# Local attention and a mixture of experts: the scores as split passes, with VectorE making the low parts

## The chip, the cores and the metric

One Trainium2 chip, one of its cores. The metric is the device time of the kernel in microseconds (us), the median of several runs.

## What is computed

x is 4 x 1024 tokens of width 512 in float32. A block of local attention with 8 heads of 128 and windows of 128 tokens is added to x and normalised; then 2 of 8 experts and a shared one are applied and normalised. Cut to the part that the change touches:

```python
q = _l2norm(q) * q_scale
k = _l2norm(k) * k_scale
kw, vw = (look_around(kb), look_around(vb))        # the window before, and this one
sim = jnp.einsum('bhnid,bhnjd->bhnij', qb * SCALE, kw)
sim = jnp.where(mask, sim, jnp.finfo(sim.dtype).min)
attn = jax.nn.softmax(sim, axis=-1)
o = jnp.einsum('bhnij,bhnjd->bhnid', attn, vw).reshape(b, H, n, DH)
```

## The kernel before

The 4096 tokens are 32 tiles of 128 tokens, each one window of the attention. Phase A (`in_steps`) runs 35 steps. In step s tile s is projected (`project`: q0, k0, q1, k1, v0, v1, each 4 heads wide, and the gates z), tile u = s-1 goes through the attention in two groups g of 4 heads, tile w = s-2 is projected out and normalised, and tile s-3 is routed. Steps 4 to 31 are a hardware loop of two steps a turn; 31 steps (1 to 31) both project and attend. Phase B then runs the experts over tiles of gathered tokens (`tile_steps`), with 64 indirect scatters of routing records on GpSimd (`scatter_records`) and 72 gathers and 72 scatters of rows.

Each engine has its own list of instructions in program order and waits on semaphores; no scheduler reorders them. The order inside a step is written out by hand in each engine's `step` function.

The projections are split: an operand a is ah + al, both in the type fp32r, and a product is three matmuls (ah,wh), (ah,wl), (al,wh) that add up in one bank (L980, and L1071 for the output). The scores (L1035) are one matmul of plain float32 a head instead, the transposed q standing (128x128) and the k of two windows moving (256 columns); the trace shows each as two records.

The path of a group of scores: VectorE scales q and k by their norms into `qkn` (`scale`, L1209), TensorE transposes 4 heads of q into bank psT[0] and 4 of k into psT[1] (`turn_qk`, L1021), ScalarE copies them into SBUF with the q scale (`heads_T`, L750 and L755), each copy raising `trev`, and TensorE's `scores` waits for

```python
                pe.wait_ge(trev, 4 * u + 2 * g + 2)
```

VectorE then adds the mask and takes the maximum (`mask_max`, L1222). The norms of the new tile run beside it on the same engines: ScalarE squares a projected bank (`squares`, L743), VectorE sums and clamps it (`sums`, L1197 and L1202), GpSimd raises it to -1/2 (`power`, L600), VectorE scales (`scale`).

TensorE's list in a full step is: project q0, turn_qk of group 0, gates (L992, 8 matmuls of 16 columns), router (L1005, 8 of the same), scores of group 0, project_out, turn_qk of group 1, project k0, scores of group 1, project q1 and k1, turn_p, project v0, values, turn_p, project v1, values, turn_x2. VectorE's is: sums and scale of q0, the router's logits, the gate sums (`add_gate`, L1255 and L1257), mask_max and gate_scale of group 0, the residual and its normalisation, sums of k0, mask_max of group 1, scale of k0, then q1 and k1, and the low parts of the output.

Of the kernel before, what the change touches and what calls it, by code (L numbers as in the profile page):

```python
# [50 lines left out]
def block_kernel(nc, x, xT, wqkvT, woT, wgT, bg, qs, ks, gateT, w13T, w2T, out):  # L51
# [7 lines left out]
    with ExitStack() as ctx:  # L59
# [3 lines left out]
        def sbuf(stack, name, shape, dt=F32):  # L63
# [47 lines left out]
        qT = sbuf(sa, "qT", [P, H, P])  # L111
        kT = sbuf(sa, "kT", [P, 2, H, P])
# [18 lines left out]
                 kT[:, :, :, :].rearrange("p s h d -> p (s h d)").rearrange("p (c n) -> p c n", n=GRP)]  # L131
# [78 lines left out]
        tr_s = sem("tr_s")  # L210
        trev = sem("trev")
# [495 lines left out]
        def _(act):  # L707
# [37 lines left out]
            def heads_T(u, g, par, middle):  # L745

                act.wait_ge(tr_s, 4 * u + 2 * g + 1)
                if middle or u >= 1:
                    act.wait_ge(sim_s, 4 * (u - 1) + 2 * g + 2)
                act.activation(qT[:, g * HPG:(g + 1) * HPG, :], psT[0][:, :], ACT.Copy, scale=qks[:, 0:1])\  # L750
                   .then_inc(trev, 1)
                act.wait_ge(tr_s, 4 * u + 2 * g + 2)
                if not middle and u == 0 and g == 0:
                    act.wait_ge(w_lo, NW)
                act.activation(kT[:, par, g * HPG:(g + 1) * HPG, :], psT[1][:, :], ACT.Copy).then_inc(trev, 1)  # L755
# [129 lines left out]
        def _(pe):  # L885
# [139 lines left out]
            def scores(u, g, first):  # L1025
                pe.wait_ge(trev, 4 * u + 2 * g + 2)
                if first and g == 0:
                    pe.wait_ge(kv_clear, 2)
                for b in range(2):
                    if not (first and g == 0):  # L1030

                        pe.wait_ge(masked, 8 * u + 4 * (g - 1) + 2 * b + 2)
                    for hh in range(2):
                        h = g * HPG + 2 * b + hh
                        mm = pe.matmul(psS[b][:, hh * 2 * P:(hh + 1) * 2 * P], qT[:, h, :], kT[:, :, h, :],  # L1035
                                       start=True, stop=True)
                    mm.then_inc(sim_s, 1)
# [121 lines left out]
        def _(dve):  # L1159
# [52 lines left out]

            def mask_max(u, g, upar, first):
# [45 lines left out]
            def first_tile():  # L1259
# [12 lines left out]
                dve.memset(kT[:, 1, :, :], 0.0).then_inc(kv_clear, 1)  # L1272
# [12 lines left out]
            def step(s, par, middle=False):  # L1285
# [18 lines left out]
                if attn_on:  # L1304
                    mask_max(u, 0, 1 - par, u_first)
                    gate_scale(u, 0, u_first)
# [11 lines left out]
                if attn_on:  # L1318
                    mask_max(u, 1, 1 - par, u_first)
# [262 lines left out]
```

## Time and profile before

| what | value |
|---|---|
| median of 3 runs | 1885.11 us (1884.11 to 1886.3) |
| span of the profiled execution | 1878.1 us |
| median less that span | 7.0 us |
| mean granted TensorE clock | 0.958 of full |
| phase A, full steps | about 60 to 1140 us of the span, 35.1 us a step |
| phase B | from about 1180 us to the end |
| score groups | 64, of 4 heads each |

The profiled execution has no time of its own beside its span; 7.0 us lie between the span and the median. A start in a timeline is in us from the start of the span, and the next figure is the duration of the row. Matmuls are pipelined and their ends are modelled, so the distance between two starts says more of a matmul's cost than its duration. What follows "<-" in brackets is what ended the idle time before a row. PE is TensorE, DVE is VectorE, ACT is ScalarE, POOL is GpSimd, SP is SyncE.

### The profile page before, as it was taken

Reading aid. Unit: us, or ns where it says so; the run is one execution under the profiler, and the core shown is the slowest. Engines: PE = TensorE matmul, PEld = TensorE weight load, DVE = VectorE, ACT = ScalarE, POOL = GpSimd, SP = SyncE. Lnnn points to the kernel's source line nnn. Section 1 sums busy time; section 2 is a strip of 40 time slices with the busy share of each in tenths; the row PEclk is TensorE's granted clock in tenths of the full one; section 3 lists DMA queues with packets and bytes.
Section 4 is the critical chain, followed back from the end, with each engine's and each line's share of the span. In section 5 each row is a group of like instructions: output and inputs, shape, how many; then the busy total and the mean of one; then the engine's idle time right before and its main releaser. Section 6 shows DMA issues by size and latency. Waiting matters only on the chain.

```text
span 1878.1 us, 28855 instructions
## 1 busy us (share of the span) xinstructions
PE 1696.8 (90%) x8566; PEld 1362.8 (73%) x8567; DVE 769.8 (41%) x1893; ACT 660.2 (35%) x1525; POOL 600.2 (32%) x689
## 2 busy tenths in 40 slices
PE   6999999999999999999999997652899999999960
PEld 4888888888888888888888886431567777777640
DVE  5444444444444444444444443621422222222386
ACT  4334334334333333333333332211323333333332
POOL 3332232232232232232232231275024444444111
PEclk8999999999999999999999998886999999999995
DMA  6000000000000000000000002452743333333697
GB/s 215 7 18 29 23 17 28 22 17 28 22 17 28 22 17 28 22 17 28 22 17 28 22 17 74 140 96 55 239 145 101 103 104 101 101 102 105 227 334 245
DMA packets 81976, 139.92 MB, mean 75 GB/s; under 512 B 10428, under 2 KB 27396, under 8 KB 81940
## 3 DMA queue, kind: packets, MB, share of 16 engines
q1 hardware_dynamic: 66852, 101.54, 16.9%
q0 software_dynamic: 13600, 37.90, 6.3%
q8 instruction: 18, 0.29, 0.1%
q10 hardware_dynamic: 1488, 0.04, 0.0%
q14 instruction: 18, 0.15, 0.0%
HBM read 97.89 MB, written 41.56 MB: 74 GB/s over the span
## 4 chain that ended last, share of the span: by engine, by line
PE 82%; issue 9%; DMA 3%; DVE 3%; ACT 1%; POOL 1%; another core or an unknown queue 0%; SPq 0%; POOLq 0%; ACTq 0%; DVEq 0%
PE bank L980 29%; PE bank L919 12%; PE bank L1071 9%; PE bank L948 7%; PE bank L1059 6%; PE bank L1035 6%; PE bank L1048 3%; PE bank L1021 3%; PE bank L894 2%; PE bank L1005 2%; PE bank L992 1%; PE bank L929 1%; DMA fs<-in_w13T 1%; DMA bx<-x_d 1%; PE bank L1078 1%
## 5 line engine op out<-in xcount | busy, mean ns | idle before, releaser
L980 PE MATMUL bank<-wh,xh 128*128 128x512 f32 x768 | 324.6, 423 | 17.7 <-DVE wl L1169 11.6
L980 PE MATMUL bank<-wl,xh 128*128 128x512 f32 x768 | 306.8, 399 | 0.0
L980 PE MATMUL bank<-wh,xl 128*128 128x512 f32 x768 | 305.1, 397 | 0.0
L600 POOL TENSOR_TENSOR rnorm<-ssmax,nhalf 128x4 f32<-128x4 f32 x128 | 131.2, 1025 | 519.9 <-DVE ssmax L1202 516.7
L606 POOL TENSOR_TENSOR pp<-pp,gs 128x1024 f32<-128x1024 f32 x64 | 121.3, 1895 | 225.9 <-DVE gs L1241 225.9
L980 PEld LDWEIGHTS bank<-wh,xh 128*128 128x128 f32 x768 | 145.9, 190 | 52.2 <-issue 11.3
L760 ACT ACTIVATE pp<-pp,nmx 128x256 f32<-128x256 f32 x256 | 127.3, 500 | 128.3 <-DVE nmx L1227 128.3
L980 PEld LDWEIGHTS bank<-wh,xl 128*128 128x128 f32 x768 | 145.8, 190 | 35.9
L743 ACT ACTIVATE sq<-bank 128x512 f32<-128x512 f32 x128 | 76.7, 599 | 257.1 <-PE bank L980 257.1
L980 PEld LDWEIGHTS bank<-wl,xh 128*128 128x128 f32 x768 | 146.4, 191 | 28.2
L1197 DVE TENSOR_REDUCE ssum<-sq 128x4 f32<-128x512 f32 x128 | 87.8, 686 | 135.6 <-ACT sq L743 132.8
L1188 DVE TENSOR_TENSOR bl<-bank,bh 128x512 fp32r<-128x512 f32 x104 | 71.8, 691 | 174.0 <-ACT bh L737 165.1
L948 PE MATMUL bank<-w2e,gT 128*128 x288 | 135.2, 592 | 0.0
L1059 PEld LDWEIGHTS bank<-pT,vv 128*128 128x128 f32 x1024 | 125.5, 194 | 9.9 <-ACT pT L769 4.7
L1209 DVE TENSOR_TENSOR qkn<-bank,rnorm 128x512 f32<-128x512 f32 x128 | 88.5, 692 | 106.7 <-POOL rnorm L600 106.7
L1059 PE MATMUL bank<-pT,vv 128*128 128x128 f32 x1024 | 126.4, 277 | 4.2 <-ACT pT L769 4.2
L1488 DVE TENSOR_TENSOR gg<-bank,gg 128x256 f32<-128x256 f32 x104 | 44.1, 424 | 205.9 <-ACT gg L867 166.1
L1246 DVE TENSOR_TENSOR ol<-bank,oh 128x512 fp32r<-128x512 f32 x64 | 44.3, 692 | 201.3 <-ACT oh L775 201.3
L1035 PE MATMUL bank<-kT,qT 128*128 128x256 f32 x512 | 123.9, 385 | 2.2 <-ACT kT L755 2.0
L894 PEld LDWEIGHTS bank<-ident,bx 128*128 128x128 f32 x416 | 52.4, 145 | 96.0 <-DMA bx<-x_d 48.6
L670 POOL DMA_INDIRECT eo_d<-eo,dstc x72 | 72.2, 1003 | 148.8 <-ACT eo L872 138.4
L775 ACT ACTIVATE oh<-bank 128x512 fp32r<-128x512 f32 x64 | 38.3, 599 | 230.6 <-PE bank L1059 230.6
(181 smaller groups left out, 3355.5 us busy)
## 6 DMA issues: line engine op xcount, KB each, us to landing
fs<-in_w13T SPq DMA_DIRECT2D x18, 512.0 KB
xt<-in_xT SPq DMA_DIRECT2D x33, 256.0 KB, 3.1
xr<-in_x SPq DMA_DIRECT2D x32, 256.0 KB, 2.7
x_d<-xr SPq DMA_DIRECT2D x32, 256.0 KB, 2.0
bx<-x_d SPq DMA_DIRECT2D x32, 256.0 KB
ga<-eo_d SPq DMA_DIRECT2D x16, 512.0 KB, 5.4
gb<-eo_d SPq DMA_DIRECT2D x16, 512.0 KB, 6.2
out<-oo SPq DMA_DIRECT2D x32, 256.0 KB, 2.7
```

Source lines behind the costliest of these rows:

```text
L600: pool.tensor_tensor(rnorm[:, :], ssmax[:, :], nhalf[:, :], ALU.pow).then_inc(rn_s, 1)
L606: pool.tensor_tensor(pp[:, g * HPG:(g + 1) * HPG, :], pp[:, g * HPG:(g + 1) * HPG, :], gs[:, g * HPG:(g + 1) * HPG].unsqueeze(2).to_broadc ...
L760: ins = act.activation(pp[:, h, :], pp[:, h, :], ACT.Exp, bias=nmx[:, h:h + 1], accum_out=esum[:, h:h + 1])
L894: mm = pe.transpose(bank[par][:, c * P:(c + 1) * P], bx[:, par, c * P:(c + 1) * P], ident[:, :])
L919: mm = pe.matmul(bank[2 + par][:, :], a[:, par, c, :], b[:, c, :], start=(c == 0 and k == 0), stop=(c == DC - 1 and k == 2))
L948: mm = pe.matmul(bank[6 + par][:, :], gT[:, par, m, :], w2[:, m, :], start=(m == 0), stop=(m == IC - 1))
L980: mm = pe.matmul(b[:, :], a[:, par, c, :], wt[:, c, cols], start=(c == 0 and k == 0), stop=(c == DC - 1 and k == 2))
L1035: mm = pe.matmul(psS[b][:, hh * 2 * P:(hh + 1) * 2 * P], qT[:, h, :], kT[:, :, h, :], start=True, stop=True)
L1059: mm = pe.matmul(psO[:, hh * P:(hh + 1) * P], vv[:, k, g * HPG + hh, :], pT[:, hh, k * P:(k + 1) * P], start=(k == 0), stop=(k == 1))
L1071: mm = pe.matmul(psY[:, :], a[:, h, :], b[:, h, :], start=(h == 0 and k == 0), stop=(h == H - 1 and k == 2))
L1197: dve.tensor_reduce(ssum[:, :], sq[:, :].rearrange("p (h d) -> p h d", d=P), AX_X, ALU.add)\
L1209: dve.tensor_tensor(qkn[:, j, :].rearrange("p (h d) -> p h d", d=P), psA[j % 2][:, :].rearrange("p (h d) -> p h d", d=P), rnorm[:, :].unsq ...
```

## The change

q and k are kept as a high and a low part of type fp32r. ScalarE's two copies now write the high parts (`qTh`, `kTh`) and raise `qk_hi`; a new function of VectorE, `heads_low`, computes the low parts from the same banks and the high parts, and raises `trev`, on which TensorE waits as before. A head's scores are three matmuls in one bank. `heads_low` stands ahead of `mask_max` in both groups. For room, the scratch for the descriptors of GpSimd's DMAs (`dynamic_dma_scratch_size`) is set to 4096 bytes, and a staging buffer that lay over kT now lies over kTh.

```diff
--- before.py
+++ after.py
@@ -108,8 +108,13 @@
         ssmax = sbuf(sa, "ssmax", [P, HPG])
         rnorm = sbuf(sa, "rnorm", [P, HPG])
         qkn = sbuf(sa, "qkn", [P, 4, GRP])
-        qT = sbuf(sa, "qT", [P, H, P])
-        kT = sbuf(sa, "kT", [P, 2, H, P])
+        qTh = sbuf(sa, "qTh", [P, H, P], F32R)
+        qTl = sbuf(sa, "qTl", [P, H, P], F32R)
+        sk = ExitStack()
+        passing_k = sbuf(sk, "passing_k", [P, DC, GRP])
+        sk.close()
+        kTh = sbuf(sa, "kTh", [P, 2, H, P], F32R)
+        kTl = sbuf(sa, "kTl", [P, 2, H, P], F32R)
         vv = sbuf(sa, "vv", [P, 2, H, P])
         pp = sbuf(sa, "pp", [P, H, 2 * P])
         mx = sbuf(sa, "mx", [P, H])
@@ -128,7 +133,7 @@
 
 
         stage = [pp[:, :, :].rearrange("p h (a c) -> p (h a c)", c=GRP // 2).rearrange("p (c n) -> p c n", n=GRP),
-                 kT[:, :, :, :].rearrange("p s h d -> p (s h d)").rearrange("p (c n) -> p c n", n=GRP)]
+                 passing_k[:, :, :]]
         stage += [passing[:, i, :, :] for i in range(4)]
         sa.close()
 
@@ -208,6 +213,7 @@
         ez_s = sem("ez_s")
         v_s = sem("v_s")
         tr_s = sem("tr_s")
+        qk_hi = sem("qk_hi")
         trev = sem("trev")
         sim_s = sem("sim_s")
         mask_s = sem("mask_s")
@@ -747,12 +753,12 @@
                 act.wait_ge(tr_s, 4 * u + 2 * g + 1)
                 if middle or u >= 1:
                     act.wait_ge(sim_s, 4 * (u - 1) + 2 * g + 2)
-                act.activation(qT[:, g * HPG:(g + 1) * HPG, :], psT[0][:, :], ACT.Copy, scale=qks[:, 0:1])\
-                   .then_inc(trev, 1)
+                act.activation(qTh[:, g * HPG:(g + 1) * HPG, :], psT[0][:, :], ACT.Copy, scale=qks[:, 0:1])\
+                   .then_inc(qk_hi, 1)
                 act.wait_ge(tr_s, 4 * u + 2 * g + 2)
                 if not middle and u == 0 and g == 0:
                     act.wait_ge(w_lo, NW)
-                act.activation(kT[:, par, g * HPG:(g + 1) * HPG, :], psT[1][:, :], ACT.Copy).then_inc(trev, 1)
+                act.activation(kTh[:, par, g * HPG:(g + 1) * HPG, :], psT[1][:, :], ACT.Copy).then_inc(qk_hi, 1)
 
             def exps(u, g):
                 act.wait_ge(nmx_s, 2 * u + g + 1)
@@ -1032,8 +1038,9 @@
                         pe.wait_ge(masked, 8 * u + 4 * (g - 1) + 2 * b + 2)
                     for hh in range(2):
                         h = g * HPG + 2 * b + hh
-                        mm = pe.matmul(psS[b][:, hh * 2 * P:(hh + 1) * 2 * P], qT[:, h, :], kT[:, :, h, :],
-                                       start=True, stop=True)
+                        for k, (a, w) in enumerate(((qTh, kTh), (qTh, kTl), (qTl, kTh))):
+                            mm = pe.matmul(psS[b][:, hh * 2 * P:(hh + 1) * 2 * P], a[:, h, :], w[:, :, h, :],
+                                           start=(k == 0), stop=(k == 2))
                     mm.then_inc(sim_s, 1)
 
             def turn_p(u, g):
@@ -1209,6 +1216,22 @@
                 dve.tensor_tensor(qkn[:, j, :].rearrange("p (h d) -> p h d", d=P),
                                   psA[j % 2][:, :].rearrange("p (h d) -> p h d", d=P),
                                   rnorm[:, :].unsqueeze(2).to_broadcast([P, HPG, P]), ALU.mult).then_inc(scaled, 1)
+
+            def heads_low(u, g, upar, first):
+
+                heads = slice(g * HPG, (g + 1) * HPG)
+                dve.wait_ge(qk_hi, 4 * u + 2 * g + 1)
+                if not first:
+                    dve.wait_ge(sim_s, 4 * (u - 1) + 2 * g + 2)
+                if first and g == 0:
+                    dve.wait_ge(qks_s, 1)
+                dve.scalar_tensor_tensor(out=qTl[:, heads, :].rearrange("p h d -> p (h d)"), in0=psT[0][:, :],
+                                         scalar=qks[:, 0:1], in1=qTh[:, heads, :].rearrange("p h d -> p (h d)").bitcast(F32),
+                                         op0=ALU.mult, op1=ALU.subtract).then_inc(trev, 1)
+                dve.wait_ge(qk_hi, 4 * u + 2 * g + 2)
+                dve.tensor_tensor(kTl[:, upar, heads, :].rearrange("p h d -> p (h d)"), psT[1][:, :],
+                                  kTh[:, upar, heads, :].rearrange("p h d -> p (h d)").bitcast(F32), ALU.subtract)\
+                   .then_inc(trev, 1)
 
             def mask_max(u, g, upar, first):
                 for b in range(2):
@@ -1269,7 +1292,8 @@
                 weight_low(7)
 
                 dve.wait_ge(w_lo, NW)
-                dve.memset(kT[:, 1, :, :], 0.0).then_inc(kv_clear, 1)
+                dve.memset(kTh[:, 1, :, :].bitcast(F32), 0.0)
+                dve.memset(kTl[:, 1, :, :].bitcast(F32), 0.0).then_inc(kv_clear, 1)
                 dve.wait_ge(consts, 11)
 
             def layernorm_stats(src, n, bn, m, v, prev):
@@ -1302,6 +1326,7 @@
                 if proj_on:
                     add_gate(s)
                 if attn_on:
+                    heads_low(u, 0, 1 - par, u_first)
                     mask_max(u, 0, 1 - par, u_first)
                     gate_scale(u, 0, u_first)
                 if out_on:
@@ -1316,6 +1341,7 @@
                 if proj_on:
                     sums(s, 1)
                 if attn_on:
+                    heads_low(u, 1, 1 - par, u_first)
                     mask_max(u, 1, 1 - par, u_first)
                 if proj_on:
                     scale(s, 1, attn_on)
@@ -1569,7 +1595,7 @@
         "w13T": w13.transpose(0, 2, 1),
         "w2T": w2.transpose(0, 2, 1),
     }
-    nc = _bacc.Bacc("TRN2", target_bir_lowering=False, num_devices=1)
+    nc = _bacc.Bacc("TRN2", target_bir_lowering=False, num_devices=1, dynamic_dma_scratch_size=4096)
     arrays, args = {}, []
     for name in _INS:
         arr = _np.ascontiguousarray(laid[name])
```

VectorE's list at group 0 of a middle step, before (`logits`, `zt` and `zb` are the router's copy and the gate sums, `pp` the masked scores):

```order
L1209 TENSOR_TENSOR qkn<-bank,rnorm 128x512
L1299 REGISTER_ALU
L1300 ISA
L1300 COPY logits<-bank 128x16
L1252 ISA
L1255 TENSOR_TENSOR zt<-bank,bgb 128x8
L1256 REGISTER_ALU
L1257 TENSOR_TENSOR zb<-bank,zt 128x8
L1217 ISA
L1218 ISA
L1222 ISA pp,mx<-bank,mask 128x256
```

and of the change:

```order
L1216 TENSOR_TENSOR qkn<-bank,rnorm 128x512
L1323 REGISTER_ALU
L1324 ISA
L1324 COPY logits<-bank 128x16
L1275 ISA
L1278 TENSOR_TENSOR zt<-bank,bgb 128x8
L1279 REGISTER_ALU
L1280 TENSOR_TENSOR zb<-bank,zt 128x8
L1225 ISA
L1228 SCALAR_TENSOR_TENSOR qTl<-bank,qks,qTh 128x512
L1231 REGISTER_ALU
L1232 TENSOR_TENSOR kTl<-bank,kTh 128x512
```

The two low parts stand behind the scaling of the new tile's q0 and behind the gate sums.

VectorE's list at group 1 of the same step, before (`xr` is the normalised residual, `ssum` and `ssmax` the sum and clamp of k0's squares):

```order
L1314 TENSOR_SCALAR xr<-xr,mv,rstd 128x512
L1194 REGISTER_ALU
L1197 TENSOR_REDUCE ssum<-sq 128x4
L1202 TENSOR_SCALAR ssmax<-ssum 128x4
L1215 REGISTER_ALU
L1217 REGISTER_ALU
L1218 REGISTER_ALU
L1222 ISA pp,mx<-bank,mask 128x256
```

and of the change:

```order
L1339 TENSOR_SCALAR xr<-xr,mv,rstd 128x512
L1201 REGISTER_ALU
L1204 TENSOR_REDUCE ssum<-sq 128x4
L1209 TENSOR_SCALAR ssmax<-ssum 128x4
L1223 REGISTER_ALU
L1225 REGISTER_ALU
L1228 SCALAR_TENSOR_TENSOR qTl<-bank,qks,qTh 128x512
L1231 REGISTER_ALU
L1232 TENSOR_TENSOR kTl<-bank,kTh 128x512
L1241 REGISTER_ALU
```

Here they stand behind the sum and the clamp of k0's squares.

## Rows read from the trace of the kernel before

**Rows 1.** The profile's page: the span, and busy time of each engine
```profile
span 1878.1 us, 28855 instructions
...
PE 1696.8 (90%) x8566; PEld 1362.8 (73%) x8567; DVE 769.8 (41%) x1893; ACT 660.2 (35%) x1525; POOL 600.2 (32%) x689
```

**Rows 2.** The page's chain that ended last, by engine
```profile
PE 82%; issue 9%; DMA 3%; DVE 3%; ACT 1%; POOL 1%; another core or an unknown queue 0%; SPq 0%; POOLq 0%; ACTq 0%; DVEq 0%
```

**Rows 3.** One step: us, busy of PE, PEld, DVE, ACT, POOL, clock, DMA share, GB/s
```profile
636.54:671.65 35.11, 35.11 (x197) 30.18 (x196) 15.85 (x46) 13.43 (x34) 10.22 (x9) 1.00 0.07 23
```

**Rows 4.** Timeline of TensorE in that step (start, duration of the row, instructions)
```profile
636.54 1.04 PE L1021 MATMUL bank<-ident,qkn 128*128 128x128 f32 x8
637.33 0.26 PE L992 MATMUL bank<-wgp,xh 128*128 128x16 f32 x1
637.44 0.26 PE L992 MATMUL bank<-wgp,xl 128*128 128x16 f32 x1
...
639.12 1.97 PE L1035 MATMUL bank<-kT,qT 128*128 128x256 f32 x8
...
650.08 1.89 PE L1035 MATMUL bank<-kT,qT 128*128 128x256 f32 x8
...
652.04 0.41 PE L980 MATMUL bank<-wl,xh 128*128 128x512 f32 x1
652.28 0.39 PE L980 MATMUL bank<-wh,xl 128*128 128x512 f32 x1
...
661.18 1.95 PE L1059 MATMUL bank<-pT,vv 128*128 128x128 f32 x16
662.97 1.04 PE L1048 MATMUL bank<-ident,pp 128*128 128x128 f32 x8
```

**Rows 5.** Timeline of VectorE, the same step
```profile
637.45 0.69 DVE L1197 TENSOR_REDUCE ssum<-sq 128x4 f32<-128x512 f32 x1 [2.02 <-ACT sq L743]
...
639.58 0.69 DVE L1209 TENSOR_TENSOR qkn<-bank,rnorm 128x512 f32<-128x512 f32 x1 [1.24 <-POOL rnorm L600]
640.19 0.16 DVE L1300 COPY logits<-bank 128x16 f32 x1
...
640.46 0.17 DVE L1257 TENSOR_TENSOR zb<-bank,zt 128x8 f32<-128x8 f32 x1
...
651.80 0.17 DVE L1202 TENSOR_SCALAR ssmax<-ssum 128x4 f32<-128x4 f32 x1
```

**Rows 6.** Timeline of ScalarE, the same step
```profile
636.82 0.60 ACT L743 ACTIVATE sq<-bank 128x512 f32<-128x512 f32 x1 [1.64 <-PE bank L980]
...
637.89 0.60 ACT L755 ACTIVATE kT<-bank 128x512 f32<-128x512 f32 x1
...
650.44 0.60 ACT L743 ACTIVATE sq<-bank 128x512 f32<-128x512 f32 x1 [2.16 <-PE bank L980]
```

**Rows 7.** Timeline of TensorE around holes; in brackets the idle before a row
```profile
18.07 0.56 PE L980 MATMUL bank<-wh,xh 128*128 128x512 f32 x1 [1.09 <-DVE zb L1257]
...
22.05 0.40 PE L980 MATMUL bank<-wl,xh 128*128 128x512 f32 x1
...
28.10 0.50 PE L980 MATMUL bank<-wh,xh 128*128 128x512 f32 x1 [2.61 <-DVE qkn L1209]
...
32.32 0.40 PE L980 MATMUL bank<-wh,xl 128*128 128x512 f32 x1
...
1144.58 3.64 PE L1059 MATMUL bank<-pT,vv 128*128 128x128 f32 x16 [3.44 <-ACT pT L769]
...
1221.05 0.66 PE L894 MATMUL bank<-ident,bx 128*128 128x128 f32 x4 [2.87 <-DMA bx<-x_d]
...
1304.30 0.69 PE L929 MATMUL bank<-ident,gg 128*128 128x128 f32 x2 [28.85 <-issue]
```

**Rows 8.** Timeline of GpSimd and of SyncE, last scatter and the read behind
```profile
1300.13 0.96 POOL L644 DMA_INDIRECT slot_d<-rec,slot_u  x1 [0.30 <-issue]
...
1361.33 0.44 SPq L527 DMA_DIRECT2D slot_t<-slot_d  x1
```

## The prediction

> **What bounds the kernel now.** I read the page's first lines first: the span is 1878.1 us and TensorE is busy for 90% of it [rows 1]. The chain that ended last is TensorE for 82% [rows 2]. An average hides which stage is full, so I cut out one step of phase A, from the transposes of one step (636.54) to those of the next (671.65). In these 35.11 us TensorE is busy for 35.11 us at the full granted clock, while VectorE has work for 15.85 us, ScalarE for 13.43 and GpSimd for 10.22 [rows 3]. So phase A is bounded by TensorE alone, with no hole in it: what is taken from TensorE shortens the kernel one for one, and every wait put on it lengthens it one for one. VectorE at 45% seems to have room. Room on average is not enough; what counts is when VectorE gets to the new work, so the last view is the step in order of time on TensorE, VectorE and ScalarE [rows 4 to 6].
>
> **Part 1: the scores on TensorE.** A group of 4 heads is now eight records of plain float32. From 650.08 to the second matmul behind it, 652.04, are 1.96 us; less the 0.24 between that one and its neighbour [rows 4], a group costs about 1.72 us. The change makes it 12 matmuls of 256 columns, each with its own load of the stationary side. No row shows this shape. From below: 16 weight-loaded float32 passes of 128x128 take 1.79 us (661.18 to 662.97), 0.112 each, and matmuls of only 16 columns still come 0.11 apart (637.33, 637.44) [rows 4], so a loaded matmul isn't faster than 0.11. From above: split matmuls of 512 columns come 0.24 apart; half their columns less is 0.107 less at 2.4 GHz, which gives 0.13. (The crude upper end, that 256 columns cost the same 0.24 as 512, would be 2.9 us a group.) I take 0.12: 1.44 us a group, a gain of 0.28, over 64 groups 18 us; with the ends 0.11 and 0.13, 26 and 10 us.
>
> The Trainium skill (TensorE: Matmul & The Clock Gate, Back-to-back issue gap) gives N/2.4 + 2.5 ns between warm matmuls, 109 ns for 256 columns. By it a group would take 1.31 us and the gain would be 26 us, 8 us more than I take; the rows show 0.24 where this rule gives 0.216 for 512 columns, so I stay with the rows.
>
> **Part 2: VectorE's two low parts, on the path.** Here lies the price. Before, the matmuls of scores waited for ScalarE's two copies only. The k copy of group 0 ended at 638.49 [rows 6], 0.63 us ahead of the scores at 639.12 [rows 4]. Now they wait for VectorE as well, and VectorE is in order: the two new instructions stand behind everything that its list has before them.
>
> Group 0: ahead of them stand the sum and the scaling of the new tile's q0 and the two gate sums. q0's squares start at 636.82 on ScalarE [rows 6], the sum at 637.45, GpSimd's power lies between, the scaling starts at 639.58, the last gate sum at 640.46 [rows 5]. So the low part of q starts at about 640.6. Its duration isn't in the trace for this operation; the nearest row is the subtraction or product over a bank of 512 columns (the scaling, 0.69 us, and the instruction behind it starts 0.61 after it, at 640.19) [rows 5]. The k part then ends at 640.6 + 0.61 + 0.69 = 641.9, and the scores start at 641.95 in place of 639.12: TensorE stands for 2.83 us.
>
> Group 1: ahead stand the sum and the clamp of k0's squares. TensorE ends k0 just as it wants the scores (650.08); the squares start at 650.44 [rows 6], the clamp at 651.80 [rows 5]. The low parts take from 651.95 to 653.22, the scores start at 653.27: 3.19 us.
>
> Both waits hang on a projection that TensorE ended just before, so they don't shrink as the step grows: the chain starts when TensorE ends q0 or k0. Nor do they hide behind other TensorE work, as it takes its list in order. What is queued behind the new VectorE instructions: the masks wait for the scores anyhow; the scaling of k0 comes later, but the third projection (q1, 2.8 us) lies between the scores and k1, which needs it. The two extra clears at the first tile cover themselves: VectorE idled before the next sum. The copies and the added DVE time (4 x 0.65 us a step) load nobody else. Low parts from above: if the product-and-subtract costs twice the subtraction, 0.7 more a group, 43 us; from below, no less than the 0.69 of a bank read of any kind, so 0.
>
> **Part 3: the clock.** TensorE's holes were none; now there are two a step. What a hole does is read from elsewhere in the trace. After 2.61 us of standing (28.10) eleven intervals take until 32.32, 4.22 us, where at the upper level they would take 11 x 0.24 = 2.64: the clock fell to 1.2 GHz and cost about 1.55. Behind the small gate matmuls and a hole of only 1.09 us (18.07) ten intervals last until 22.05: 3.98 for 2.40, again 1.55. After 3.44 us the sixteen records of 1144.58 take 3.64, where the same sixteen at 661.18 take 1.95. But after 2.87 us (1221.05) the four transposes behind it take 0.66, full speed [rows 4, 7]. Group 0's hole follows upon 1.8 us of those same small matmuls, so I count 1.55 for each; group 1's follows dense work, where the rows go both ways, more often down: 1.1.
>
> **Part 4: the smaller DMA scratch.** It holds GpSimd's descriptors. The last of the 64 record scatters starts at 1300.13, and what they wrote is read at 1361.33 [rows 8]: should they wait for the smaller scratch, there are 60 us of cover. Yet while they ran TensorE stood for 28.85 us until 1304.30, put down to "issue" [rows 7]. I can't say what of it hangs on the scratch: 0 taken, with a bound of 29 us either way.
>
> **Sum.** A step of the 31 that both project and attend: 2.83 + 3.19 of waits, 1.55 + 1.1 of clock, 2 x 0.28 gained: +8.1 us, 251 us in all. The last attention step has no projections: its two groups wait one more VectorE instruction each, 2 x 0.7, less 0.56: +1. Span 1878.1 + 252 = 2130. The median of the runs, 1885.11, is 7.0 above the profiled span, which I take as what lies around it; the forecast is **2137 us**, about 13% slower.
>
> **The rivals.**
> (a) The waits come, the clock holds, as behind the hole of 1221.05: 31 x 2.65 = 82 us less, 2055. For it: that row, and that dense work stands on both sides. Against: three of the four holes under 4 us [rows 7]. Chance 0.15.
> (b) The other side: VectorE reaches the low parts in time, and the gain of part 1 is all there is. Point of decision: both must be done by 639.1 and 650.1, so started by 637.8 and 648.8. Then 1885 - 18 = 1867. Against: the scaling alone starts at 639.58, and the order of VectorE's list puts it first. It needs a reordering that the built program doesn't have. Chance 0.03.
> (c) Each of the 12 loads lies bare: 0.107 of columns plus the 0.11 of a load is 0.22 a matmul, 2.6 us a group, 0.9 more than now; against my sum 64 x 1.17 = 75 us more, 2212. Against: in the 512-column row only 0.03 of the 0.24 is not columns, so a load hides almost wholly there. Chance 0.03. The Trainium skill (same page, The mechanism, on packing) says a weight load overlaps a running matmul only when it goes to another row group, which speaks for this rival; the row speaks against it.
> (d) The scratch or its shift of the stretch around 1300 adds another such stand: 29 us, 2166. Chance 0.08.
> (e) The low-part work is dearer or a hole lowers the clock for longer: 2150 to 2185. Chance 0.1.
> The change does what it says: both lists show it.
> The forecast itself has 0.6, a no-change case 0.01. The range 2050 to 2185 takes in (a), (d) and (e) and leaves out (b), (c) and ends of both, some 0.15. A measurement of this kernel tells 0.2% from no change. Slower by more than that: 0.95; faster 0.03; same 0.02.
>
> **What would show it.** In the profile after: the scores groups as 12 matmuls about 0.12 apart at full clock (0.11 to 0.13 right; over 0.15 wrong); idle of TensorE before them of about 2.8 and 3.2 us a step, released by VectorE's subtraction into kTl, some 185 us in all; VectorE busy about 85 us more; the granted clock of a step below 1.00, near 0.92; a step of about 43 us in place of 35.11. A step of 40.6 at clock 1.00 is rival (a); one of under 35.1 is (b). The forecast is wrong if TensorE's idle in phase A stays under 100 us, or if phase B moves by more than 10 us.

## The result, and the profile after

The changed kernel takes 2160.49 us at the median of 4 runs (2154.81 to 2165.45), against 1884.61 for the kernel before beside it: a ratio of 1.148, with a 95% interval of 1.1448 to 1.1513. It is 14.8% slower; forecast were 2137 us and 13%.

The page's head, TensorE's busy time and the chain that ended last, which answer to [rows 1, 2], and a group of the new scores (mean ns of one; idle before it and what ended the idle):

```profile
span 2163.7 us, 29559 instructions
...
PE 1815.8 (84%) x8822; PEld 1466.8 (68%) x8823; DVE 860.0 (40%) x2022; ACT 658.6 (30%) x1525; POOL 602.3 (28%) x689
...
PEclk8898989898998989898998989978889999999995
...
PE 47%; issue 32%; DVE 8%; POOL 4%; DMA 4%; ACT 2%; another core or an unknown queue 1%; POOLq 0%; DVEq 0%; SPq 0%; ACTq 0%
...
L1042 PE MATMUL bank<-kTh,qTh 128*128 128x256 f32 x256 | 106.7, 417 | 186.9 <-DVE kTl L1232 186.9
```

TensorE's share falls from 90% to 84%, the row of granted clocks alternates between 8 and 9 through all of phase A, and 186.9 us of idle stand before the first pass of the scores, all ended by VectorE's subtraction into kTl.

One step of phase A by stretch, against [rows 3], and a longer stretch (length, busy us of PE, PEld, DVE, ACT, POOL, then the clock):

```profile
705.50:748.01 42.51, 36.49 (x205) 31.43 (x204) 18.58 (x50) 13.39 (x34) 10.21 (x9) 0.96 0.06 20
60.00:1370.00 1310.00, 1138.81 (x6036) 981.22 (x6037) 545.43 (x1458) 395.91 (x1007) 302.98 (x267) 0.90 0.06 18
```

This step, one of the short ones, is 42.51 us in place of 35.11, with TensorE busy for 36.49 of it. Over phase A the clock is 0.90.

The timeline of TensorE in that step, against [rows 4]:

```profile
705.50 1.03 PE L1027 MATMUL bank<-ident,qkn 128*128 128x128 f32 x8
...
707.97 0.26 PE L1011 MATMUL bank<-wgp,x2l 128*128 128x16 f32 x1
711.01 0.38 PE L1042 MATMUL bank<-kTh,qTh 128*128 128x256 f32 x1 [2.79 <-DVE kTl L1232]
...
726.66 0.38 PE L1042 MATMUL bank<-kTh,qTh 128*128 128x256 f32 x1 [3.23 <-DVE kTl L1232]
726.88 0.27 PE L1042 MATMUL bank<-kTl,qTh 128*128 128x256 f32 x1
726.99 0.28 PE L1042 MATMUL bank<-kTh,qTl 128*128 128x256 f32 x1
727.11 0.28 PE L1042 MATMUL bank<-kTh,qTh 128*128 128x256 f32 x1
727.23 0.28 PE L1042 MATMUL bank<-kTl,qTh 128*128 128x256 f32 x1
```

and that of VectorE, against [rows 5]:

```profile
708.53 0.69 DVE L1216 TENSOR_TENSOR qkn<-bank,rnorm 128x512 f32<-128x512 f32 x1 [1.23 <-POOL rnorm L606]
...
709.41 0.17 DVE L1280 TENSOR_TENSOR zb<-bank,zt 128x8 f32<-128x8 f32 x1
709.53 0.75 DVE L1228 SCALAR_TENSOR_TENSOR qTl<-bank,qks,qTh 128x512 fp32r<-128x512 f32 x1
710.20 0.68 DVE L1232 TENSOR_TENSOR kTl<-bank,kTh 128x512 fp32r<-128x512 f32 x1
...
724.98 0.17 DVE L1209 TENSOR_SCALAR ssmax<-ssum 128x4 f32<-128x4 f32 x1
725.18 0.75 DVE L1228 SCALAR_TENSOR_TENSOR qTl<-bank,qks,qTh 128x512 fp32r<-128x512 f32 x1
725.85 0.68 DVE L1232 TENSOR_TENSOR kTl<-bank,kTh 128x512 fp32r<-128x512 f32 x1
```

Both holes stand where the forecast put them. Group 0's low parts start at 709.53, just behind the gate sum, and end at 710.88; the scores start at 711.01 after 2.79 us of idle. Group 1's start at 725.18 behind the clamp of k0's squares and end at 726.53; the scores start at 726.66 after 3.23 us. At full clock the passes come 0.12 us apart (726.88 to 727.23); only the second stands 0.22 behind the first.

What the clock did, in the next step:

```profile
753.37 0.58 PE L1042 MATMUL bank<-kTh,qTh 128*128 128x256 f32 x1 [2.64 <-DVE kTl L1232]
...
754.17 0.41 PE L1042 MATMUL bank<-kTh,qTh 128*128 128x256 f32 x1
754.39 0.41 PE L1042 MATMUL bank<-kTl,qTh 128*128 128x256 f32 x1
...
758.65 0.63 PE L1078 MATMUL bank<-woh,oh 128*128 128x512 f32 x1
759.08 0.47 PE L1078 MATMUL bank<-wol,oh 128*128 128x512 f32 x1
759.39 0.40 PE L1078 MATMUL bank<-woh,ol 128*128 128x512 f32 x1
...
769.95 0.58 PE L1042 MATMUL bank<-kTh,qTh 128*128 128x256 f32 x1 [3.03 <-DVE kTl L1232]
...
773.01 0.40 PE L986 MATMUL bank<-wl,xh 128*128 128x512 f32 x1
```

The passes behind the hole of 2.64 us come 0.21 apart and the matmuls of 512 columns 0.43 apart, until 759.4: the level of 1.2 GHz for some 6 us. Behind the second hole of this step it lasts until about 772.9; in the step above it did not fall behind the second at all (0.12 apart at once).

The first 6.25 us behind the two holes of three steps in a row (columns as above; the clock is the third figure from the end):

```profile
711.01:717.26 6.25, 6.25 (x26) 5.52 (x27) 2.02 (x11) 2.08 (x8) 0.00 (x0) 0.73 0.00 0
726.66:732.91 6.25, 6.25 (x33) 5.33 (x34) 3.10 (x12) 1.66 (x6) 0.06 (x1) 1.00 0.00 0
753.37:759.62 6.25, 6.25 (x21) 5.49 (x22) 1.73 (x10) 2.08 (x8) 0.00 (x0) 0.53 0.00 0
769.95:776.20 6.25, 6.25 (x27) 5.61 (x28) 2.33 (x10) 0.34 (x1) 0.00 (x0) 0.77 0.00 0
798.13:804.38 6.25, 6.25 (x22) 5.55 (x23) 1.72 (x9) 2.08 (x8) 0.00 (x0) 0.56 0.00 0
814.67:820.92 6.25, 6.25 (x21) 5.53 (x22) 2.33 (x10) 0.00 (x0) 0.00 (x0) 0.52 0.00 0
```

At a mean clock of 0.73 the work of 0.27 x 6.25 = 1.7 us is lost. So counted, group 0's hole cost 1.7, 2.9 and 2.8 us of clock in these steps and group 1's 0, 1.4 and 3.0: 2.5 and 1.5 on average (estimates from these rows). Read over all 29 steps in the middle of phase A, the clock was at the low level behind group 0's hole in each of them, for 3.4 to 6.1 us, and behind group 1's in 19, for 2.8 to 6.2 us.

Where the 285.6 us of span went (2163.7 less 1878.1): TensorE's count of the choices, the first matmul of phase B, starts at 1474.5 in place of 1181.3, so phase A took 293.2 us more, and phase B 689.2 in place of 696.8, 7.6 less. The mean distance of two steps (start of group 0's transposes to the next, 29 of them) is 44.34 us against 35.12: 9.22 a step, 286 over 31. The other 7 lie at the edges. The medians lie 275.9 us apart (2160.49 less 1884.61), 10 less than the spans: the profiled execution of the changed kernel was the slowest of its four (2165.45 us), that of the kernel before the fastest of its four (1879.85).

### The profile page after: what moved, and what is told of

Same layout as the page of the kernel before. It is cut to its first block, busy times and chain, and to the rows that moved or that the text cites. A ratio compares the mean times of both kernels' runs of the same rounds, so it can differ in the third digit from the quotient of the medians.

```text
span 2163.7 us, 29559 instructions
## 1 busy us (share of the span) xinstructions
PE 1815.8 (84%) x8822; PEld 1466.8 (68%) x8823; DVE 860.0 (40%) x2022; ACT 658.6 (30%) x1525; POOL 602.3 (28%) x689
## 4 chain that ended last, share of the span: by engine, by line
PE 47%; issue 32%; DVE 8%; POOL 4%; DMA 4%; ACT 2%; another core or an unknown queue 1%; POOLq 0%; DVEq 0%; SPq 0%; ACTq 0%
PE bank L925 11%; PE bank L1078 10%; PE bank L1042 7%; PE bank L986 7%; PE bank L954 7%; POOL rnorm L606 3%; DVE kTl L1232 2%; PE bank L900 2%; PE bank L1027 1%; DVE ssum L1204 1%; DMA z_d<-eo 1%; DMA fs<-in_w13T 1%; DVE qkn L1216 1%; ACT sq L749 1%
## 5 line engine op out<-in xcount | busy, mean ns | idle before, releaser
L986 PE MATMUL bank<-wl,xh 128*128 128x512 f32 x768 | 313.6, 408 | 0.0
L986 PE MATMUL bank<-wh,xl 128*128 128x512 f32 x768 | 310.5, 404 | 0.0
L1042 PE MATMUL bank<-kTh,qTh 128*128 128x256 f32 x256 | 106.7, 417 | 186.9 <-DVE kTl L1232 186.9
L1042 PEld LDWEIGHTS bank<-kTh,qTh 128*128 128x128 f32 x256 | 72.8, 285 | 203.3 <-issue 178.3
L986 PEld LDWEIGHTS bank<-wh,xh 128*128 128x128 f32 x768 | 152.3, 198 | 50.6 <-issue 11.3
L986 PEld LDWEIGHTS bank<-wh,xl 128*128 128x128 f32 x768 | 150.6, 196 | 37.5
L986 PEld LDWEIGHTS bank<-wl,xh 128*128 128x128 f32 x768 | 152.1, 198 | 29.3
L1245 DVE CUSTOM_DVE_ANT_0 pp<-bank,mask 128x256 f32<-128x256 f32 x256 | 97.7, 422 | 139.8 <-PE bank L1042 139.6
L925 PE MATMUL bank<-w13h,bh 128*128 x288 | 119.1, 414 | 0.0
```

What stands on the lines that cost most here:

```text
L925: mm = pe.matmul(bank[2 + par][:, :], a[:, par, c, :], b[:, c, :], start=(c == 0 and k == 0), stop=(c == DC - 1 and k == 2))
L986: mm = pe.matmul(b[:, :], a[:, par, c, :], wt[:, c, cols], start=(c == 0 and k == 0), stop=(c == DC - 1 and k == 2))
L1042: mm = pe.matmul(psS[b][:, hh * 2 * P:(hh + 1) * 2 * P], a[:, h, :], w[:, :, h, :], start=(k == 0), stop=(k == 2))
```

## The experiments

Theory: VectorE's place in its list makes two holes a step, and the holes lower the clock; the passes alone are a gain. Rivals: the passes or their loads cost; VectorE's load as such costs, wherever it stands; the scratch does something. The step figures are means over 28 or 29 steps of phase A, measured as above; which ones are taken moves a mean by up to 0.1 us. Holes are the idle before the first pass of the scores, mean of the steps that have one. The kernel before took between 1864 and 1887 us on the chips used, so times are told as ratios to it on the same chip.

| run | ratio (95% interval) | step, us | holes of group 0 and 1, us | phase B, us |
|---|---|---|---|---|
| before | 1 | 35.12 | none | 696.8 |
| changed | 1.148 (1.1448 to 1.1513) | 44.34 | 2.73, 3.12 | 689.2 |
| changed, again | 1.1604 (1.1583 to 1.1625) | 44.34 | 2.73, 3.12 | 683.3 |
| scratch alone | 1.0017 (1.0005 to 1.0028) | 35.12 | none | 685.3 |
| high parts only | 0.9958 (0.9941 to 0.9974) | 34.66 | none | 690.3 |
| holes filled | 1.099 (1.0965 to 1.1014) | 40.77 | filled; 0.12, 0.19 left in every second step | 688.3 |
| both moved | 1.0193 (1.0169 to 1.0218) | 35.85 | 0.33, none | 685.6 |
| group 0 moved | 1.1026 (1.1002 to 1.105) | 40.97 | 0.33, 3.12 | 683.3 |
| group 1 moved | 1.0792 (1.0771 to 1.0812) | 39.35 | 2.73, none | 682.0 |
| first heads first | 0.9981 (0.9967 to 0.9995) | 34.61 | none | 683.5 |
| both moved, two fillers | 1.0003 (0.9986 to 1.002) | 35.11 | none | 685.1 |
| kernel before, again | 1.0023 (1.0004 to 1.0042) | 35.12 | none | 693.3 |
| kernel before, large scratch, third chip | 1.0013 (0.9999 to 1.0027) | 35.12 | none | 699.3 |
| kernel before, small scratch, third chip | 0.9948 (0.993 to 0.9966) | 35.12 | none | 686.0 |

The kernel before against itself gives 1.0023 and 1.0013, so a ratio within 0.2 to 0.3% of 1 is no difference here.

**The passes alone.** ScalarE's copies raise `trev` as before the change, and all three passes use the high parts; the correction terms are left out.

```diff
-                        for k, (a, w) in enumerate(((qTh, kTh), (qTh, kTl), (qTl, kTh))):
+                        for k, (a, w) in enumerate(((qTh, kTh), (qTh, kTh), (qTh, kTh))):
...
-                    heads_low(u, 0, 1 - par, u_first)
...
-                    heads_low(u, 1, 1 - par, u_first)
```

> The changed kernel without its low parts: VectorE computes none, ScalarE's copies release TensorE as before the change, and the three passes all use the high parts (so the correction terms of the scores are left out). It shows the passes alone. My theory: 12 passes 0.119 us apart, a group 0.27 us cheaper, steps of 34.6 us and 1885 - 17 = 1868 us, no hole, clock 1.00. Rival (passes or their weight loads cost more than the rows before showed): 1885 us or more.

Steps of 34.66 us, a ratio of 0.9958. The passes gain 0.46 us a step, and phase B starts at 1166.5, 14.7 us earlier. By the starts a group is 0.30 us cheaper (0.60 a step), and every second step does last 34.53 us; the others last 34.79, as about 0.25 us more pass between two matmuls of 512 columns behind the scores of group 1. So the 12 loaded passes cost no more than the records that they replace; the whole loss is elsewhere, and the rival of bare weight loads falls.

**The holes filled.** Matmuls that nobody reads stand in the holes, written to psY between its last read and `project_out`.

```diff
+            def fill(s, par, taken, n):
+                if taken is not None:
+                    pe.wait_ge(res_s, taken)
+                for c in range(n):
+                    pe.matmul(psY[:, :], xh[:, par, c % DC, :], wh[:, c % DC, 0:GRP], start=True, stop=True)
...
+                if proj_on and out_on:
+                    fill(s, par, None if w_first else w, 11)
                 if attn_on:
                     scores(u, 0, u_first)
...
                     project(s, "k0", par, first, route_on)
+                if proj_on and out_on:
+                    fill(s, par, w + 1, 13)
```

> The changed kernel with matmuls of 512 columns that nobody reads put into its two holes of a step: 11 ahead of the scores of group 0 (2.6 us) and 13 ahead of those of group 1 (3.0 us), from step 2 on. TensorE waits as long as before for the low parts, but works meanwhile. My theory (holes of 6 us a step, and some 3.7 us a step more because the clock falls behind them): granted clock 1.00 in a step, steps of 40.6 to 40.9 us, 2160 - 115 = 2045 us. Rival (the clock costs nothing by itself, all of it is wait): no gain, 2160 us or slower.

Busy time and clock by stretch in this run (columns as above):

```profile
60.00:1300.00 1240.00, 1232.47 (x6916) 1044.81 (x6917) 558.69 (x1506) 407.45 (x1036) 313.22 (x276) 1.00 0.06 19
```

Clock 1.00 (the changed kernel: 0.90), steps of 40.77 us, phase B from 1366.6 on, 108 us earlier. TensorE waits for the same low parts, only busy. So of the 9.2 us a step some 3.6 are the clock: that is how much comes back when the same time is worked through. The rest is the wait.

**Both low parts moved.** The same instructions, earlier in VectorE's list (the calls at their old places are taken out; that is not shown).

```diff
+                if attn_on:
+                    heads_low(u, 0, 1 - par, u_first)
                 if proj_on:
                     sums(s, 0)
...
                     layernorm_stats(xr[:, par, :], w, bn_s, mv_s, ve_s, None if w_first else rstd_s)
+                    if attn_on:
+                        heads_low(u, 1, 1 - par, u_first)
                     dve.wait_ge(rstd_s, w + 1)
```

> The changed kernel with the same instructions, but VectorE's two low parts earlier in its list: in group 0 first in the step, ahead of the sum and the scaling of q0; in group 1 inside the normalisation of the residual, while that waits for GpSimd. My theory (the place in the list is the price, not the work): hole of group 0 about 0.3 us, of group 1 none, clock 1.00, steps of 34.9 us, 1878 us, below the kernel before. Rival (88 us more VectorE work loads the step wherever it stands): above 1900 us.

Ratio 1.0193: seven eighths of the loss are gone, with VectorE doing exactly the same work. The rival of VectorE's load is far off, but I missed too: expected were steps of 34.9 us, measured 35.85, in turns of 35.0 and 36.75. In the long ones (TensorE's timeline):

```profile
440.20 0.38 PE L1042 MATMUL bank<-kTh,qTh 128*128 128x256 f32 x1 [0.36 <-DVE kTl L1232]
...
440.53 0.28 PE L1042 MATMUL bank<-kTh,qTl 128*128 128x256 f32 x1
...
441.09 0.41 PE L1042 MATMUL bank<-kTh,qTh 128*128 128x256 f32 x1
441.31 0.41 PE L1042 MATMUL bank<-kTl,qTh 128*128 128x256 f32 x1
...
444.08 0.50 PE L1078 MATMUL bank<-wol,oh 128*128 128x512 f32 x1
444.41 0.40 PE L1078 MATMUL bank<-woh,ol 128*128 128x512 f32 x1
```

The hole is only 0.36 us, but from 440.9 on the passes come 0.21 apart (441.09, 441.31) and the matmuls of 512 columns 0.43 (442.37 to 442.80), until 444.4. The holes are of 0.30 and 0.36 us in turn. The 5 us behind two of each kind (the clock is the third figure from the end):

```profile
440.20:445.20 5.00, 5.00 (x21) 4.45 (x22) 3.27 (x15) 0.30 (x1) 1.01 (x1) 0.66 0.00 0
476.89:481.89 5.00, 5.00 (x28) 4.40 (x29) 3.28 (x15) 0.36 (x1) 1.01 (x1) 1.00 0.00 0
548.63:553.63 5.00, 5.00 (x21) 4.26 (x22) 3.29 (x15) 0.35 (x1) 1.01 (x1) 0.66 0.00 0
585.32:590.32 5.00, 5.00 (x28) 4.39 (x29) 3.28 (x15) 0.30 (x1) 1.01 (x1) 1.00 0.00 0
```

Up to 512 us of the span the clock fell behind the holes of 0.36 us alone (440.20), from 548 us on behind those of 0.30 alone (548.63). So it isn't the larger of the two sizes that lowers it. A hole of 0.3 us behind the 16 small gate and router matmuls seems enough; the next run tests that.

**The tiny hole filled.** Two matmuls of 512 columns ahead of group 0's scores; VectorE's list as in the last run.

```diff
+                if proj_on and out_on:
+                    fill(s, par, None if w_first else w, 2)
                 if attn_on:
                     scores(u, 0, u_first)
```

> The kernel with both low parts moved, and two matmuls of 512 columns that nobody reads ahead of the scores of group 0 (0.47 us). VectorE's list is that of the run with both moved. My theory (the hole of 0.36 us behind the small gate matmuls lowers the clock there in every second step, 0.8 us a step): no hole, clock 1.00, steps of 34.69 + 0.47 = 35.15 us at most, 0.7 us less than with the hole, ratio 1.007. Rival (the 0.8 us come from VectorE's later masks, not from the clock): steps of 35.85 to 36.0 us, ratio 1.02 or more.

Steps of 35.11 us, in turns of 35.0 and 35.2. The long steps of 36.75 are gone although 0.47 us of work were added, so it was the hole and the clock, not VectorE's later masks. (The 34.69 in the expectation should be 34.66.) The ratio, 1.0003, is below the 1.007 that I expected; phase B, 685.1 us against 693.3 for the kernel before on this chip, is 8 us of that difference.

**First heads first.** Both low parts moved as above, and no useless work: TensorE's list of a group starts with passes that need ScalarE's copies alone, and takes k's low part last (`part` issues one pass of head `hh` of a pair).

```diff
-                pe.wait_ge(trev, 4 * u + 2 * g + 2)
+                pe.wait_ge(qk_hi, 4 * u + 2 * g + 2)
...
                 for b in range(2):
                     if not (first and g == 0):
                         pe.wait_ge(masked, 8 * u + 4 * (g - 1) + 2 * b + 2)
...
+                    part(b, 0, qTh, kTh, 0)
+                pe.wait_ge(trev, 4 * u + 2 * g + 1)
+                for b in range(2):
+                    part(b, 0, qTl, kTh, 1)
+                pe.wait_ge(trev, 4 * u + 2 * g + 2)
+                for b in range(2):
+                    part(b, 0, qTh, kTl, 2)
+                    for k, (a, w) in enumerate(((qTh, kTh), (qTh, kTl), (qTl, kTh))):
+                        mm = part(b, 1, a, w, k)
+                    mm.then_inc(sim_s, 1)
```

> Both low parts moved as in the run with both moved, and TensorE's list of a score group begins with what needs no low part: the high-high pass of the first head of either bank as soon as ScalarE's copies are there, then their pass with q's low part, and only then k's low part. 0.48 us of matmuls stand ahead of the wait for it. Same arithmetic in another order. My theory (in that run the hole of 0.3 us behind the small gate matmuls was what lowered the clock and made steps of 35.0 and 36.75 us): no hole, clock 1.00, steps of 34.6 us as with the passes alone, a ratio of 0.995. Rival (the alternate slow steps come from VectorE's later masks or from its work on the banks): steps still 35.9 us in the mean, a ratio of 1.02.

```profile
60.00:1120.00 1060.00, 1057.88 (x6235) 916.26 (x6234) 550.50 (x1500) 410.14 (x1041) 311.26 (x275) 1.00 0.07 23
```

Clock 1.00, steps of 34.61 us, ratio 0.9981 (0.9967 to 0.9995): the change with both orders put right is level with the kernel before, and the best complete version with the change in it. In the steps it keeps the gain of the passes (0.5 us each, 16 us in all); in the time, 0.2% is no more than the kernel before shows against itself. I had expected 0.995. Of the 16 us some 6 are lost again in the first step that attends, 36.3 us in place of 29.9: there the moved low parts still make TensorE wait (1.77 and 1.56 us before passes of the scores).

**One group at a time.** Of the two moves on VectorE's list above, the first run has group 0's alone (again without the lines at the old place):

```diff
+                if attn_on:
+                    heads_low(u, 0, 1 - par, u_first)
                 if proj_on:
                     sums(s, 0)
```

and the second group 1's alone:

```diff
                     layernorm_stats(xr[:, par, :], w, bn_s, mv_s, ve_s, None if w_first else rstd_s)
+                    if attn_on:
+                        heads_low(u, 1, 1 - par, u_first)
```

> The changed kernel with the low parts of group 0 alone first in VectorE's list of a step; those of group 1 stay behind k0's clamp. My theory (each hole is set by what stands ahead of its low parts): hole of group 0 about 0.3 us, of group 1 3.2 us as in the changed kernel. Clock: in the run with both moved the 0.3 us behind the small gate matmuls lowered the clock in every second step for 3.0 us (1.3 us lost); a hole of 3.2 us in dense work cost 0 to 2.6. So steps of 39.5 to 40.2 us, a ratio to before of 1.076 to 1.087. Rival (the two waits are one: VectorE has a fixed lateness, which comes out at group 1 if it is saved at group 0): hole of group 1 over 4 us, steps over 41.5.

> The changed kernel with the low parts of group 1 alone moved into the normalisation of the residual; those of group 0 stay behind the scaling of q0. My theory: hole of group 0 2.7 us, of group 1 none; behind that hole the clock falls in every step, for 3 to 5.3 us (1.4 to 2.4 us lost), as in the changed kernel. Steps of 38.9 to 39.7 us, a ratio of 1.063 to 1.076. Rival (the clock falls behind a hole in dense work alone, and group 0's falls in the changed kernel come from group 1's hole): clock 1.00, steps of 37.3 us.

The holes don't depend on one another: 2.73 stays 2.73 and 3.12 stays 3.12 when the other goes. The price of the clock does depend. With group 0's hole alone a step has 39.35 - 34.66 - 2.73 = 1.96 us beyond the passes and the hole; the step is as expected, and its ratio, 1.0792, is a little over the 1.076. With group 1's alone (and the tiny one) it has 40.97 - 34.66 - 0.33 - 3.12 = 2.86; step and ratio (1.1026) lie over the 39.5 to 40.2 and 1.076 to 1.087 that I expected. Together that would be 4.8 us; in the changed kernel, which has both holes, it is 3.8 (below). With group 1's hole alone the clock fell behind it in every full step, in all but one for 5.6 to 5.9 us; in the changed kernel it didn't fall there in 10 of 29. Behind one of them (the last line is the 6 us from its first pass):

```profile
426.15 0.57 PE L1042 MATMUL bank<-kTh,qTh 128*128 128x256 f32 x1 [3.23 <-DVE kTl L1232]
...
426.74 0.41 PE L1042 MATMUL bank<-kTh,qTl 128*128 128x256 f32 x1
426.95 0.41 PE L1042 MATMUL bank<-kTh,qTh 128*128 128x256 f32 x1
...
426.15:432.15 6.00, 6.00 (x21) 5.31 (x22) 2.33 (x10) 0.00 (x0) 0.00 (x0) 0.53 0.00 0
```

**The changed kernel again,** on the chip of the first experiments.

> The changed kernel once more, on the chip of the experiments, where the kernel before took 1865 us at the median in place of 1885. If those 20 us lie in phase B (the transfers), phase A has the same holes (2.8 and 3.2 us) and steps of 44.3 us, and the time is 2140 to 2150 us. If they lie in phase A, the steps differ.

2159.06 us, holes as before to a hundredth, steps within 0.1 us. My 2140 to 2150 missed: the changed kernel did not get faster on that chip, only the kernel before. That difference isn't in phase A, as the kernel before with the smaller scratch has its steps of 35.12 us there too (next run). Where else it lies is not shown: no profile of the kernel before was taken on that chip.

**The scratch.** Alone, put on the kernel before:

```diff
-    nc = _bacc.Bacc("TRN2", target_bir_lowering=False, num_devices=1)
+    nc = _bacc.Bacc("TRN2", target_bir_lowering=False, num_devices=1, dynamic_dma_scratch_size=4096)
```

> The kernel before with the smaller DMA scratch alone. My theory: the scratch costs nothing, 1885 us within 0.3%, steps of 35.1 us, and the stand of some 29 us among the record scatters stays as it was. Rival (the scratch, or what it shifts, matters in phase B, where the changed kernel was 7 us shorter): the span from the count of choices to the end differs from before by 5 us or more.

1.0017, so no gain on that chip, and phase A as it was. But there was no stand like the 28.85 us of [rows 7], against my theory. I went after it with the kernel before and its profile on another chip (no edit), and then with both, the kernel before and the same with the line above, side by side on a third.

> The kernel before once more, with a profile on the chip of the experiments. If the larger scratch causes the stand of 28.85 us among the scatters, it is in this profile too, at 1250 to 1310 us, and phase B (from the count of choices to the end) takes 697 us as in the first profile. If the stand is the chip's or that one execution's, it is gone, phase B takes 683 to 686 us as with the smaller scratch, phase A is unchanged (steps 35.12 us), and the time is 1865 us.

There the stand was again (28.58 us), phase B 693.3; the kernel with two fillers, on the same chip, had 685.1 and no such stand.

> The kernel before with the smaller scratch, beside the kernel before on the same chip, five rounds. So far: two profiles with the large scratch have a stand of 28.6 to 28.9 us among the scatters and a phase B of 693 to 697 us, the profiles with the small one have no such stand and 683 to 690 us, but on other chips in part. Theory 1 (the scratch sets the pace of the scatters and with it the stand): no stand over 13 us here, phase B of 685 us, 5 to 10 us less than with the large one. Theory 2 (the chip, not the scratch): both alike.

> The kernel before, with its profile on the same chip as the run with the smaller scratch. Theory 1: a stand of some 28 us, phase B of 693 us or more, time 5 to 10 us above the run with the small scratch. Theory 2: phase B within 3 us of that run, with or without a stand.

On one chip: small scratch 0.9948, phase B 686.0 us; large scratch 1.0013, phase B 699.3. GpSimd's scatters and TensorE's longest stand, first with the small scratch:

```profile
1217.73 1.12 POOL L644 DMA_INDIRECT slot_d<-rec,slot_u  x1 [4.30 <-DVEq L1425]
...
1319.64 0.96 POOL L644 DMA_INDIRECT slot_d<-rec,slot_u  x1 [0.30 <-issue]
...
1247.28 1.11 PE L894 MATMUL bank<-ident,bx 128*128 128x128 f32 x4 [8.87 <-DMA bx<-x_d]
```

then with the large one:

```profile
1215.34 1.12 POOL L644 DMA_INDIRECT slot_d<-rec,slot_u  x1 [4.30 <-DVEq L1425]
...
1298.11 0.96 POOL L644 DMA_INDIRECT slot_d<-rec,slot_u  x1 [0.30 <-issue]
...
1274.41 0.69 PE L929 MATMUL bank<-ident,gg 128*128 128x128 f32 x2 [12.71 <-issue]
...
1300.58 1.22 PE L948 MATMUL bank<-sh,gT 128*128 128x512 f32 x1 [20.42 <-issue]
```

With the small scratch the 64 scatters are spread over 101.9 us, with the large over 82.8 (the starts of the first and the last), and in the latter TensorE stands for 12.71 and 20.42 us before it can go on, put down to "issue". The scratch does pace the scatters: in all the profiles here, on several chips, they are spread over 82.7 to 84.0 us with the large scratch (three profiles) and over 101.6 to 108.4 with the small one (eleven). On this chip the small one was worth 0.5 to 0.6%. All three profiles with the large scratch have stands of 20 to 29 us in this stretch, none with the small one has over 13. Why the other engines stand while GpSimd scatters undisturbed I have not shown, nor why the gain was missing on the chip of the first experiments, where the kernel before had no profile.

## Why the prediction was right, and where not

- **The bound.** Right: TensorE had no slack, and the waits show one for one in the step.
- **Part 1, the passes.** Right: forecast 0.12 us apart, measured 0.118 (the passes from 726.88 on); 0.28 us a group forecast, 0.30 by the starts and 0.23 by the mean step with the passes alone (0.46 a step).
- **Part 2, the holes.** Right in place and size: 2.83 and 3.19 forecast for that step, 2.79 and 3.23 in the one shown, 2.73 and 3.12 on average; 187 us of idle forecast for the 31 full steps, 182 measured in them; that the page has 186.9 is luck, for 5.2 of it belong to the last attention step. The low part of q is slightly dearer than a subtraction, 0.75 us against 0.69. That both holes are set by VectorE's list and not by its load is shown by moving each.
- **Part 3, the clock.** Right in kind, too small: forecast 1.55 + 1.1 = 2.65 us a step, measured 9.22 - 5.85 + 0.46 = 3.83; the filled holes give back 3.6. The mis-sized term is the price of a fall, 1.55 us. It came from two rows of the first tile, where the low level cost some 1.6 us each (3.98 for 2.40, 4.22 for 2.64). In the changed kernel it lasts for up to 6.2 us behind a hole. By the windows of three steps above, group 0's hole cost 2.5 where I had 1.55, and group 1's 1.5 where I had 1.1 (together 4.0, against 3.83 by the steps), so most of the error lies in group 0. Nor do the prices add: each hole alone costs 1.96 and 2.86, both together 3.83, since the clock doesn't fall behind group 1's hole in every step when group 0's is there. My sum took each hole by itself. That is (3.83 - 2.65) x 31 = 37 us of what was missed.
- **The last attention step.** Wrong: I gave it +1 us with one more VectorE instruction a group. With no k0 to project, group 1's low parts stand behind the whole normalisation of the residual and the hole is 3.64 us; group 0's is 1.52. That is part of the 7 us at the edges; which other stretches make up the rest I have not shown.
- **Part 4, the scratch.** I took 0 within 29 us; it is -7.6 us of span in phase B in the first pair of profiles, -13 in the pair on one chip, and nothing in one comparison of times (1.0017). The sign was open, and it is a gain where it is anything.
- **The sum.** 252 us of span forecast, 285.6 measured: holes -5, passes +3, clock +37, edges +6, scratch -8, with rounding. The median lies 3.2 us below the profiled span, where I had put it 7.0 above. The 7.0 was not what lies around a span: the profiled execution of the changed kernel took 1.8 us more than its span (2165.45 for 2163.7), as do the others here, and by the same measure that of the kernel before is the one of 1879.85 us. The other 5.3 were the distance of one quick execution from the median. The forecast of the time, 2137, is off by 23 us and that of the span by 34; the 10 us between the two are luck.
- **The rivals.** (a), the clock holds: refuted, 0.90. (b), the low parts come in time: not this kernel, but the version with first heads first comes out there, at 0.9981. Its point of decision held in the run with both moved: there group 0's low parts came some 0.3 us late, and that much TensorE stood. (c), bare loads: refuted by the passes alone. The rule on the overlap of weight loads behind it, in the Trainium skill (TensorE: Matmul & The Clock Gate, The mechanism), would have made a group 2.6 us by my estimate; measured were about 1.43 (12 x 0.119), so loads of full rows do hide behind running matmuls here. (d), another stand from the scratch: the other way round. Of the two prices of a pass the 0.12 from the rows was right. The Trainium skill (TensorE: Matmul & The Clock Gate, Back-to-back issue gap) has 0.109 by a formula that it gives for a matmul by itself, and these each carry a weight load.

## What to carry to other kernels

When TensorE has no slack, a cheap instruction on an idle engine costs what stands ahead of it in that engine's list. Read the list at the new place, name the row that it will stand behind, and ask where the same work could stand: here the same low parts cost 15% at one place and 2% at another, and nothing once TensorE's own list began with passes that need none of them. And count a hole in TensorE's work twice, once for the wait and once for the clock behind it. The price of the clock is that of all the holes together (here 3.8 us a step for two, 2.0 and 2.9 for each alone). Put work that is needed anyway into the hole, or shrink it to nothing: the useless matmuls brought the clock back but not the wait.

## What was not expected of the hardware

- A hole of 0.30 or 0.36 us behind 16 matmuls of 16 columns lowers the clock in every second step, for 3.4 us (35.85 us a step in the mean). It fell first behind the larger holes alone and from 548 us on behind the smaller alone. Without the hole (34.61 us a step) or with two dense matmuls in it (35.11) the clock stays at 1.00. The same small matmuls without a hole never lowered it in a full step, nor did the holes of 0.12 and 0.19 us that were left between dense matmuls in the filled run.
- Behind a hole of 3.0 to 3.2 us in dense work the low level lasts for anything from nothing to 6.2 us. It depends on the other hole of the step: with it the level did not fall in 10 of 29 steps, without it it fell in all. The steps of the changed kernel are of three kinds, 42.1 to 42.5, 44.6 to 45.0 and 45.9 to 46.5 us, most often in turn.
- With a smaller descriptor scratch the 64 scatters are slower (101.9 us in place of 82.8) and the kernel is not: on one chip it was 0.5% faster, and the stands of 20 us or more of the other engines were not there. What ties the two together is not shown.
